# Another order of the slots: a pair's first products two batches behind it in place of three

## What is computed

```python
def xattn(q, k, v, gamma):          # q = layernorm(x); k = v = ctx, 8 heads of 16 channels
    qk = jnp.einsum('bhdq,bhdl->bhql', qh, kh) * scale
    sm = jax.nn.softmax(qk, axis=-1)
    ret = jnp.einsum('bhql,bhdl->bhdq', sm, vh)
    return gamma * ret.reshape(B, Dv, Lq)

def ffn(x, Wg, W0a, b0a, W0b, b0b, W1a, b1a, W1b, b1b):
    top_expert = jnp.argmax(softmax(einsum('bsh,eh->bse', x, Wg)), axis=-1)
    out0 = einsum('bsf,hf->bsh', gelu(einsum('bsh,fh->bsf', x, W0a) + b0a), W0b) + b0b
    out1 = einsum('bsf,hf->bsh', relu(einsum('bsh,fh->bsf', x, W1a) + b1a), W1b) + b1b
    mask0 = (top_expert == 0)[..., None]
    return out0 * mask0 + out1 * (1 - mask0)

x = x + xattn(layernorm(x), ctx, ctx, gamma)
x = x + ffn(layernorm(x), ...)
```

## Time and profile before

| what | value |
|---|---|
| median of 3 runs (lowest, highest) | 233.05 us (232.84, 233.07) |
| profiled execution, device time | 232.91 us |
| its span in the trace | 231.1 us |
| TensorE busy | 217.1 us (94%) |
| VectorE busy | 174.3 us (75%) |
| ScalarE busy | 145.6 us (63%) |
| GpSimd busy | 137.8 us (60%) |

### The profile page before, as it was taken

How to read it: one execution, slowest core, us unless ns; L and a number is a source line. 1 busy time by engine, 2 the same in 40 slices (tenths; PEclk the granted TensorE clock), 3 DMA queues, 4 the chain that set the end, 5 groups by cost and what they waited for, 6 DMA issues and landing times.

```text
span 231.1 us, 5325 instructions
## 1 busy us (share of the span) xinstructions
PE 217.1 (94%) x2036; PEld 165.9 (72%) x2041; DVE 174.3 (75%) x357; ACT 145.6 (63%) x220; POOL 137.8 (60%) x180
## 2 busy tenths in 40 slices
PE   7789879788999999999999999999999999899995
PEld 3334445456787978788787978797879787778995
DVE  7499977999579976997699869994888444545583
ACT  6205766856985597658784779477944986624240
POOL 6852314879889718972698358934762287382800
PEclk9999999999999999999999999999999999999999
DMA  4785499543224340625052704250302000000101
GB/s 136 244 301 185 140 372 375 176 142 139 92 85 150 113 143 16 240 67 191 4 198 74 237 1 119 94 180 33 72 1 72 0 27 3 23 26 0 47 3 45
DMA packets 19393, 26.40 MB, mean 114 GB/s; under 512 B 1992, under 2 KB 12840, under 8 KB 19112
## 3 DMA queue, kind: packets, MB, share of 16 engines
q1 hardware_dynamic: 18942, 25.66, 33.4%
q10 hardware_dynamic: 426, 0.40, 0.5%
HBM read 11.01 MB, written 2.10 MB: 57 GB/s over the span
## 4 chain that ended last, share of the span: by engine, by line
PE 76%; DVE 8%; ACT 5%; DMA 4%; issue 3%; SPq 3%; POOL 1%
PE ff L775 20%; PE ff L795 12%; PE od L722 11%; PE st L710 10%; PE ff L807 7%; PE smax L697 5%; DVE nmax L396 3%; PE od L730 3%; DMA qkst<-mlow 2%; PE od L737 2%; PE tr L748 2%; ACT P L576 2%; PE tr L758 2%; DMA qkst<-parts 1%; PE od L679 1%
## 5 line engine op out<-in xcount | busy, mean ns | idle before, releaser
L576 ACT ACTIVATE P<-st 128x1024 f32<-128x1024 f32 x64 | 66.1, 1033 | 47.7 <-PE st L710 47.3
L396 DVE TENSOR_REDUCE nmax<-smax 128x4 f32<-128x1024 f32 x56 | 68.5, 1224 | 21.3 <-PE smax L697 20.5
L267 POOL TENSOR_TENSOR mv<-mv,power 128x1 f32<-128x1 f32 x32 | 19.1, 596 | 47.9 <-DVE mv L378 47.8
L775 PE MATMUL ff<-xnTh,w1h 128*128 128x256 f32 x128 | 38.1, 298 | 1.0 <-DVE y L495 1.0
L775 PE MATMUL ff<-xnTl,w1h 128*128 128x256 f32 x128 | 36.0, 281 | 0.0
L775 PE MATMUL ff<-xnTh,w1l 128*128 128x256 f32 x128 | 35.9, 281 | 0.0
L285 POOL TENSOR_TENSOR hidL<-hid,hidH 128x1024 fp32r<-128x1024 f32 x13 | 31.0, 2386 | 6.0 <-DVE hidH L457 4.6
L609 ACT ACTIVATE hid<-ff,b1t 128x256 f32<-128x256 f32 x64 | 26.1, 479 | 12.2 <-PE ff L775 12.1
L710 PE MATMUL st<-qkst 64*128 64x256 f32 x256 | 32.2, 330 | 1.4 <-ACT P L576 0.5
L795 PE MATMUL ff<-w2h,hidH 128*128 128x256 f32 x124 | 32.1, 292 | 0.0
L722 PE MATMUL od<-P,vt 128*32 128x256 f32 x512 | 30.9, 382 | 0.0
(11 more groups left out here) (81 smaller groups left out, 369.6 us busy)
## 6 DMA issues: line engine op xcount, KB each, us to landing
qkst<-parts SPq DMA_DIRECT2D x47, 256.0 KB
xv<-in_xv SPq DMA_DIRECT2D x16, 256.0 KB, 3.0
qk<-in_qk SPq DMA_DIRECT2D x15, 256.0 KB, 3.1
out<-y SPq DMA_DIRECT2D x16, 128.0 KB, 2.7
w1t<-in_w SPq DMA_DIRECT2D x1, 1024.0 KB, 7.2
w2t<-in_w SPq DMA_DIRECT2D x1, 1024.0 KB, 7.9
qkst<-parts ACTq DMA_DIRECT2D x1, 256.0 KB
qkst<-mlow SPq DMA_DIRECT2D x16, 8.0 KB
```

Source lines behind the costliest of these rows:

```text
L267: pool.tensor_tensor(mv[:, b % 2, 11:12], mv[:, b % 2, 10:11], power[:, 0:1], ALU.pow).then_inc(s_rstd, 1)
L396: dve.tensor_reduce(nmax[:, c % 2, :, :, j].rearrange("p a e -> p e a"), (ff if c in WIDE and j % 2 else smax)[:, :, :, :], AX.X, ALU.max, ...
L576: act.activation(P[:, b % 2, j, :, :, :].rearrange("p e a l -> p (e a l)"), st[:, :, :, :].rearrange("p e a l -> p (e a l)"), ACT.Exp, sca ...
L775: mm = pe.matmul(ff[:, u // 2 % 2, u % 2, :], w[:, a, e, m * 128:(m + 1) * 128], xs[:, i % 2, a, :], start=a == 0 and n == 0, stop=a == LC ...
```

## The change

The slots in which each engine issues its operations are laid out anew. The batches alternate in a cycle of two:

- In an odd batch b of 3 or more TensorE begins pair i = (b - 3) / 2: slot 0 `transpose_x(b-2)`, from batch 5 on `high_pass(b-4,1)` and `low_pass(b-4,1)`, `gemm1` units 0 to 3; slot 1 `values(b-1)`, units 4 and 5; slot 2 `transpose_od(b-1)`, units 6 and 7; slot 3 `transpose_att(b-1)`, `high_pass(b-3,0)`, `low_pass(b-3,0)`.
- In an even batch b: slot 0 `values(b-1)`; slot 1 `transpose_od(b-1)`, `high_pass(b-4,1)`; slot 2 `transpose_att(b-1)`, `high_pass(b-3,0)`, `low_pass(b-4,1)`, `transpose_x(b-2)`; slot 3 `low_pass(b-3,0)`.
- Attention's chain of batch b-1 is issued within batch b (before, `transpose_att` and what follows were issued one batch later). VectorE, ScalarE and GpSimd follow: `residual`, `moments2` and the second `rstd` go to slots 2 and 3 of the same batch, `x_norm` to slot 3 of even and slot 0 of the next even batch, both `final` of a pair to slot 0 of an odd batch, both `gate` to slot 1 of an odd batch, `masks` and `add_bias` both for b-3 to slot 2.
- Pair 6 is then begun in the loop, and only pair 7 wholly in the tail.
- Spins remain in slots 6, 7, 9, 10 and 11 in place of 6, 7, 8, 10, 11, 12, 14 and 15 (those up to slot 4 are kept).
- `gemm1` and `high_pass` of the first pair wait for one expert's low weights each; `w1l` is made expert by expert. `gate(b)` waits for the `gate` before it.

The core of the diff:

```diff
-SPIN = {..., 6: 3, 7: 3, 8: 3, 10: 3, 11: 3, 12: 3, 14: 3, 15: 3}
+SPIN = {..., 6: 3, 7: 3, 9: 3, 10: 3, 11: 3}
 # GpSimd
+                if j == 0 and b >= 4 and not odd:
+                    low_hidden((b - 4) // 2, 1)
+                if j == 1 and b >= 3 and odd:
+                    low_hidden((b - 3) // 2, 0)
                 for c in prepared(n):
                     rstd(c, mv1, c + 1, s_var1, s_rstd1)
-                if j == 0 and b >= 5 and b % 2:
-                    low_hidden((b - 5) // 2, 1)
-                if b >= 4 and j == 3 and b % 2 == 0:
-                    low_hidden((b - 4) // 2, 0)
+                if j == 3 and b >= 1 and odd:
+                    rstd(b - 1, mv2, b - 1 + 1, s_var2, s_rstd2)
+                if j == 2 and b >= 2 and not odd:
+                    rstd(b - 1, mv2, b - 1 + 1, s_var2, s_rstd2)
...
-                if j == 0 and b >= 2:
-                    rstd(b - 2, mv2, b - 1, s_var2, s_rstd2)
-                if j == 2 and b >= 2:
-                    masks(b - 2)
-                if j == 2 and b >= 3:
+                if b >= 3 and j == 2:
+                    masks(b - 3)
                     add_bias(b - 3)
 # VectorE
+                if j == 0 and b >= 3 and odd:
+                    if b >= 5:
+                        final(b - 5)
+                    low_xT(b - 2)
+                    if b >= 5:
+                        final(b - 4)
                 if c < B:
                     take_max(c, k)
+                if j == 1 and b >= 3 and odd:
+                    gate(b - 3)
+                    high_gelu((b - 3) // 2)
+                if j == 1 and b >= 2 and not odd:
+                    normalise(b - 1)
+                if k == 0 and 2 <= c <= B:
                     max_parts(c - 1)
                 for p in prepared(n):
                     moments1(p)
+                if j == 1 and b >= 3 and odd:
+                    gate(b - 2)
+                if j == 2 and odd and b >= 1:
+                    normalise(b - 1)
+                if j == 2 and b >= 2 and not odd:
+                    residual(b - 1)
+                    moments2(b - 1)
                 for p in prepared(n - 1):
                     q_norm(p)
+                if j == 3 and odd and b >= 1:
+                    residual(b - 1)
+                    moments2(b - 1)
+                if j == 3 and b >= 2 and not odd:
+                    x_norm(b - 1)
+                    low_xT(b - 2)
+                if j == 0 and b >= 2 and not odd:
                     x_norm(b - 2)
 # ScalarE
+                if j == 0 and first:
+                    high_xT(b - 2)
+                if j == 1 and first:
+                    for u in range(4):
+                        if u == 2 and c <= B:
+                            copy_max(c - 1)
+                        hidden((b - 3) // 2, u)
+                if j == 2 and first:
+                    for u in range(4, 6):
+                        hidden((b - 3) // 2, u)
                 if b >= 0:
                     exp(b, j)
...
+                if b >= 1 and j == (1 if odd else 0):
                     copy_od(b - 1)
 # TensorE
+                    if j == 0 and b >= 3:
+                        transpose_x(b - 2, b + 1)
+                        if b >= 5:
+                            high_pass(b - 4, 1)
+                            low_pass(b - 4, 1)
                         for u in range(0, 4):
+                            gemm1(i, u)
...
+                    if j == 3:
+                        if b < 3:
+                            pe.wait_ge(s_xTl, b - 1)
+                            spin(tr[:, :, :, :], SPIN.get(n, 0))
+                        if b >= 4:
+                            low_pass(b - 3, 0)
```

More of the change, by code:

```diff
@@ L360, in _ @@
                     pool.tensor_tensor(w2l[:, units, :], w2t[:, units, :], w2h[:, units, :], ALU.subtract).then_inc(s_w2l, 1)
-            rstd(B - 2, mv2, B - 1, s_var2, s_rstd2)
-            masks(B - 2)
+            masks(B - 3)
             add_bias(B - 3)
[L364 to L368, removed]
+            rstd(B - 1, mv2, B - 1 + 1, s_var2, s_rstd2)
+            for b in (B - 2, B - 1):
+                masks(b)
+                add_bias(b)
         @block.vector
@@ L630, in _ @@
                 c, k = divmod(n + LEAD, PAIRS)
[L631 to L636, removed]
+                odd = b % 2 == 1
+                first = b >= 3 and odd
+                if j == 0 and first:
+                    high_xT(b - 2)
+                if j == 1 and first:
+                    if b == 3:
+                        act.wait_ge(s_bias, 32)
+                    for u in range(4):
[5 more added lines that the diff above has]
+                        hidden((b - 3) // 2, u)
                 if b >= 0:
@@ L831, in _ @@
                     transpose_max(0, 0)
+                odd = b % 2 == 1
                 if k == 0 and 2 <= c <= B:
-                    transpose_max(c - 1, max(0, b - 2))
-                even = b >= 4 and b % 2 == 0
-                odd = b >= 5 and b % 2
-                if j == 0:
-                    if b >= 2:
-                        transpose_att(b - 2)
-                    if even:
-                        for u in range(0, 4):
-                            gemm1((b - 4) // 2, u)
-                    if odd:
-                        low_pass(b - 5, 0)
-                        high_pass(b - 5, 1)
@@ L865, in _ @@
-                if j == 3 and b >= 1:
-                    if b < 4:
+                    transpose_max(c - 1, max(0, b - 1 if odd else b - 2))
+                if odd and b >= 1:
+                    i = (b - 3) // 2
+                    if j == 0 and b >= 3:
[3 more added lines that the diff above has]
+                            low_pass(b - 4, 1)
+                        for u in range(0, 4):
+                            gemm1(i, u)
+                    if j == 1:
+                        if b == 1:
+                            pe.wait_ge(s_vones, 2)
+                        values(b - 1)
+                        if b >= 3:
+                            for u in range(4, 6):
+                                gemm1(i, u)
+                    if j == 2:
@@ L867, in _ @@
                         pe.wait_ge(s_ods, b)
                         spin(od[:, :], SPIN.get(n, 0))
-                    transpose_od(b - 1)
-                    if even:
-                        high_pass(b - 4, 0)
-                    if odd:
-                        high_pass(b - 4, 1)
-                        low_pass(b - 4, 1)
-            transpose_att(B - 2)
-            for u in range(0, 4):
-                gemm1(B // 2 - 2, u)
+                        transpose_od(b - 1)
+                        if b >= 3:
+                            for u in range(6, 8):
+                                gemm1(i, u)
@@ L887, in _ @@
             transpose_x(B - 1, B)
-            for b in (B - 4, B - 3):
-                high_pass(b, 1)
-                low_pass(b, 1)
             for u in range(UNITS):
```

129 lines of the change are left out of this document (54 added, 75 removed).

## The result

| what | before | forecast | after |
|---|---|---|---|
| median | 233.01 us | 239.0 | 248.06 us (246.72 to 248.95, 4 runs) |
| span of the profiled execution | 231.1 us | 237.2 | 246.3 us |

The ratio is 1.0642 (95% interval 1.0607 to 1.0676): 15.1 us slower, where 6.1 were forecast. The direction was right, the size too small, and the range (to 241.5) missed it.

What follows compares the result with a forecast made beforehand. TensorE was taken as the bound, full from slot 16 to 56, with VectorE having only 4 us of room. The terms -0.55 + 1.7 + 3.0 + 1.9 = +6.1 us on 232.91 gave 239.0 us, range 235.0 to 241.5.

Steps and rivals of the forecast that it cites:

- the 8.0: TensorE work moved ahead of slot 16: slot 16 may start 8.0 us later without loss if the tail shortens equally.
- Steps 1 and 2: Batches 1 to 3: VectorE's chain delays slot 12 by 2.6 us, batch 3's empty time is mostly used; together -0.55 us.
- Step 3: GpSimd in batches 3 and 4: its last w2l comes late and TensorE idles in slot 17; +1.7 us.
- Step 4: Two-batch cycle: VectorE's even-batch run outlasts TensorE's work, so a cycle takes 25.05 us; +3.0 us in all.
- Step 5: Tail from slot 56 to the last pair's first product: 3.6 us of gaps, partly from final; +1.9 us.
- Removed spins count nothing by themselves: Spins taken out of the loop cost no time, since they stood where TensorE waited anyway.
- rival 3: The clock falls after TensorE's 3.3 us idle before slot 12: +1.4 to +3, giving 240.5 to 242 us; chance 0.15.
- A granted clock under 1.00 after slot 11: Listed among the signs that would show the prediction wrong; no size given.
- rival 2: The chains of steps 3 and 4 are partly hidden and cost half or less: 234.5 to 236.7 us; chance 0.18.
- batch 3's 3.8 empty us: TensorE time in batch 3 without work, 1.7 us idle and about 2.1 us of spins, which the new order fills.

Runs made afterwards that it cites:

- experiment 1: The changed kernel (after) with 13 spin products added in slot 11 before TensorE's wait for low_xT(0): 242.91 us, ratio 1.0424.
- experiment 12: Experiment 6 with experiment 8's GpSimd order, ten tail spins; slot 11's wait and 13 spins replaced by 6 spins there and 4 in slot 12: 235.49 us.
- experiment 10: The kernel before without its 24 spins in slots 6 to 15: 236.27 us, ratio 1.0139.
- experiment 5: After with 13 spins in slot 11, all w2l subtractions in slot 12, and even batches' moments1 one slot earlier, before x_norm: 246.10 us, ratio 1.0556.
- experiment 6: Experiment 5 with GpSimd's low_hidden(i, 1) moved to slot 1 of the even batch, behind rstd: 239.79 us, ratio 1.0267.
- experiment 3: After with GpSimd's four w2l subtractions all issued in slot 12, ahead of low_hidden(0,0): 243.23 us, ratio 1.044.
- experiment 8: After with 13 spins in slot 11, all w2l subtractions in slot 12, and GpSimd's pad_values and masks before even batches' second rstd: 239.90 us, ratio 1.0314.

## Why the prediction was too low

The stages of the profiled executions, in us, cut at the starts of slots 16, 24, 48 and 56 and at the last pair's first product:

| stage | before | forecast | after | experiment 1 (clock 1.00) | experiment 12 |
|---|---|---|---|---|---|
| to slot 16 | 55.00 (63.00 with the 8.0) | 62.45 | 66.75 | 62.67 | 61.97 |
| 16 to 24 | 24.73 | 27.11 | 28.72 | 27.23 | 24.88 |
| 24 to 48 | 73.10 | 75.15 | 76.74 | 76.76 | 74.65 |
| 48 to 56 | 24.37 | 24.61 | 25.03 | 25.62 | 24.79 |
| 56 to last `gemm1` | 39.62 (31.62) | 33.55 | 33.20 | 33.22 | 33.20 |
| to the end | 14.28 | 14.3 | 15.86 | 14.30 | 14.31 |
| span | 231.1 | 237.2 | 246.3 | 239.8 | 233.8 |

- **Steps 1 and 2 were right** as far as waits go: 62.45 against 62.67 in experiment 1. Inside the sum two errors cancel, which is luck: `x_norm(1)` holds VectorE for 1.00 us, not 0.33, beside GpSimd's `w1l`, and the chain starts at 40.05, not at 40.55. The first pair has 60 products by the start of batch 4 in the code and in the trace (48, 8 and 4), not 72; the 7.8 us of the prediction fit 60. What is 4.1 us more in after is the clock.
- **Step 3 was right**: the late `w2l` is there, and taking it away gives 2.2 us in slots 16 to 20. In after a fall follows it, 1.5 us more.
- **Step 4 was 2.6 us short** from slot 24 to slot 56 (102.38 in experiment 1 for 99.76). The mechanism is the forecast one: with `moments1` out of the run the cycle is 25.04. The way from the maxima product to the transpose is 7.94 us in after (98.35 to 106.29) for 7.68, and `final` holds `gemm1` for 0.37, which the step had only as a bound. In batch 12 `x_norm` takes 1.27 us beside GpSimd's `chosen` in experiment 1 and lays open 1.06 us; in after it takes 0.40, and the stage is 0.6 us shorter.
- **Step 5 was right**, 0.35 less than forecast: the idles in front of `transpose_x(15)` and of the last `gemm1` are 1.27 and 0.93 us, where it had 1.5 and 1.0.
- **The failed step is the clock.** The sum puts it at nothing, and two statements fell. "Removed spins count nothing by themselves": experiment 10 puts 3.3 us on the 24 spins in the kernel before (no run prices the 12 that the change took out). And rival 3 was put aside at 0.15 and sized at 1.4 to 3 us. A granted clock under 1.00 after slot 11 was named as a sign of being wrong, and it came. Experiment 1 and after differ by 6.5 us of span, in three places: 4.1 up to slot 16, 1.5 in slots 16 to 20, 1.6 at the end, less 0.6 from batch 12. Rival 3 counted one fall that lasts through 24 products; the first fall alone lasts 10.2 us (47.2 to 57.4), and two more came behind gaps that steps 3 and 5 themselves forecast. The evidence for the mechanism stood in the prediction: the idle of 3.3 us was forecast, and so was what products cost at 1.2 GHz. (The spins of the earlier trace rows, which rival 3 sets beside it, begin about 0.33 us apart at first, but the granted clock over them is 1.00 in the trace, so they don't show the lower level.) The first fall's 4.1 us are shown by experiment 1, which takes out the gap and nothing else. For the other two only their size is shown: experiment 1 has their gaps and not the falls.
- **The range** runs to 235.0 and 241.5, where the middles of rivals 2 and 3 are 235.6 and 241.25; it changes nothing.

The Trainium skill (TensorE: Matmul & The Clock Gate, section "HAM oscillation — how this bites in real kernels") says that a gap makes the next group start cold. This trace agrees for the gap of 3.54 us. The case of that section, a long wait, isn't that of experiment 10, whose clock is down with no gap over 1.44 us ahead of it; there the measurement goes further than the section.

So of the 15.2 us between the profiled executions 6.5 are the clock and 8.7 are waits, of which 6.1 were forecast. The expected gain, batch 3's 3.8 empty us filled, shows in slot 16's start (61.97 in experiment 12 for 63.00). It is eaten by the cycles (about 0.5 us each, four times, and 0.15 in the first) and by the tail (1.6): -1.0 + 0.15 + 2.0 + 1.6 = 2.7 us, which is experiment 12's span over that of before. What remains in each cycle are two idles of 0.31 and 0.32 us on TensorE; what would remove them wasn't tried. Why the clock falls behind the same gap in one execution and not in the next stays open.

## What to carry to other kernels

When an order leaves TensorE idle, price the idle twice: once for itself, and once for the slower clock that may follow it; products without use at such a place are part of the schedule and are moved with it. When a VectorE instruction is moved, look at what GpSimd runs at the new time, since its duration there can be a multiple of the one in the trace. With the clock at 1.00 (experiment 1) the forecast of the queue orders was good to 0.4 us in four of six stages, in one of them by luck, and 0.4 to 1.0 us a cycle too low in the loop.

## What the runs showed of the hardware

- **VectorE and GpSimd exclude each other for some instructions.** `x_norm` (one input and one output of 128 x 256 float32 in SBUF) takes 0.41 us alone, 0.93 beside `low`, 1.27 beside `chosen` and 2.52 when `low_hidden` (2.38) started 0.02 ahead of it. `gate`, with two inputs in SBUF, goes from 0.42 to 1.71. `take_max`, which reads PSUM, keeps its mean of 1.22 us. It works the other way round too: in the tail of after VectorE's `low_relu` starts 0.04 us ahead of GpSimd's two instructions of `masks`, and these take 1.58 us for 0.40 (timelines of VectorE and GpSimd).

```profile
220.59 1.23 DVE L463 TENSOR_TENSOR hidL<-hid,hidH 128x1024 fp32r<-128x1024 f32 x1 [0.58 <-ACT hidH L609]
```

```profile
220.63 1.58 POOL L290 TENSOR_SCALAR mask<-lead 128x1 f32<-128x1 f32 x2
```

The Trainium skill (SBUF — State Buffer, section "SBUF: two separate sides") has this as an exclusive lock on a shared pair of ports, held by whoever starts first for the whole instruction. The rows agree in that `x_norm` and `gate`, where they are long, end 0.15 to 0.3 us behind GpSimd's instruction; experiments 5 and 6 are the test. They don't show who wins when both start within 0.1 us: `x_norm` starts 0.08 us ahead of `chosen` in experiment 1 and takes 1.27, and 0.09 ahead of it in after and takes 0.40, while `chosen` takes 1.21 for 1.04.

- **The clock can go down without a long gap, and the gap alone doesn't say when.** In experiment 10 it fell with no idle over 1.44 us ahead. Among the profiled executions the gap of 1.06 us at slot 52 was followed by a fall in three of six, the pair of gaps of 1.27 and 0.93 us in the tail in four of nine (after and experiments 3, 6 and 8). Both executions with the gap of 3.54 us (after, experiment 3) have the long fall of 10 us. In experiment 8 the clock also fell in slot 12, for 3.4 us, although 13 spins stood in slot 11.
